# Routed experts of a four-layer decoder: weight buffers addressed by block number, token numbers copied in halves

## The reference

```python
# layer 0: 16 experts, 6 chosen, inner width 176
scores = softmax(h @ gate_w.T); topk_w, topk_idx = top_k(scores, 6)
for e in range(16):
    out = silu(h @ w_gate[e].T) * (h @ w_up[e].T) @ w_down[e].T
    y = y + cw[:, e:e + 1] * out          # cw: the weight of e for each token, 0 where it isn't chosen
# layer 2: 8 experts, 2 chosen, inner width 176, and a shared expert of width 704 with a sigmoid gate
# layer 3: 64 experts, 4 chosen, inner width 96, weights normalised over the chosen
```

## Time and profile before

| | us |
|---|---|
| median of 3 runs (lowest, highest) | 2009.03 (2002.38, 2015.11) |
| profiled execution, its own time | 2001.86 |
| its span, first to last instruction | 2000.0 |
| TensorE busy | 1134.1 |
| VectorE busy | 1150.5 |
| GpSimd busy | 573.5 |
| ScalarE busy | 474.0 |
| mean granted TensorE clock | 0.81 |
| DMA moved | 196.52 MB, 98 GB/s over the span |

### The profile page before, as it was taken

The page is one execution under the profiler, slowest core; times in us unless marked ns, Lnnn a source line. Parts: engine busy times, 40 slices in busy tenths (PEclk is TensorE's granted clock), DMA queues, the critical chain, the costliest instruction groups (busy, mean ns, idle before and its releaser), DMA issues. The chain is left out here.

```text
span 2000.0 us, 21530 instructions
## 1 busy us (share of the span) xinstructions
PE 1134.1 (57%) x5620; PEld 709.2 (35%) x5620; DVE 1150.5 (58%) x2019; ACT 474.0 (24%) x881; POOL 573.5 (29%) x578
## 2 busy tenths in 40 slices
PE   5325537887035773552597803698647278647760
PEld 2201124555023551111354602575424134425550
DVE  5759974333345446898976595421357478483333
ACT  2143301221002344330211100332121156312220
POOL 0026603331730111762200073033212032014425
PEclk9669967999567895897798856899878589869985
DMA  6024334886305502341000011205600510267863
GB/s 203 0 87 147 105 107 139 247 258 213 105 21 128 64 2 87 115 136 63 0 1 0 0 12 31 86 1 150 190 24 0 155 38 3 67 186 231 234 189 102
DMA packets 146194, 196.52 MB, mean 98 GB/s; under 512 B 35056, under 2 KB 109955, under 8 KB 145485
## 3 DMA queue, kind: packets, MB, share of 16 engines
q1 hardware_dynamic: 109996, 144.47, 24.4%
q0 software_dynamic: 12608, 31.26, 5.8%
q10 hardware_dynamic: 23520, 19.93, 3.1%
HBM read 153.55 MB, written 41.75 MB: 98 GB/s over the span
## 5 line engine op out<-in xcount | busy, mean ns | idle before, releaser
L163 PE MATMUL psum<-w_ident,h 128*128 128x128 f32 x144 | 32.7, 422 | 183.3 <-DVE h L144 183.3
L453 PE MATMUL psum<-l0s_conv_out,w_ident 128*128 128x512 f32 x128 | 65.0, 633 | 83.4 <-DVE l0s_conv_out L550 83.4
L453 PE MATMUL psum<-l1s_conv_out,w_ident 128*128 128x512 f32 x128 | 65.3, 636 | 80.0 <-DVE l1s_conv_out L550 80.0
L1471 DVE TENSOR_REDUCE l3x_neg<-psum 128x2 f32<-128x512 f32 x128 | 80.9, 684 | 49.5 <-PE psum L1343 49.5
L925 PE MATMUL psum<-l0f_w_in,l0f_xT 128*128 128x352 f32 x224 | 82.1, 491 | 26.1 <-issue 12.2
L163 PEld LDWEIGHTS psum<-w_ident,h 128*128 128x128 f32 x144 | 29.1, 223 | 186.7 <-DVE h L144 174.5
L175 ACT ACTIVATE hT<-psum 128x512 f32<-128x512 f32 x40 | 21.7, 595 | 304.4 <-PE psum L163 262.7
L1446 ACT ACTIVATE l3x_work<-psum 128x512 f32<-128x512 f32 x128 | 72.5, 599 | 65.3 <-PE psum L1365 65.0
L419 POOL TENSOR_TENSOR l1s_xpad<-l1s_du,l1s_bc 128x1024 f32<-128x1024 f32 x32 | 75.3, 2353 | 32.5 <-DVE psum L546 32.3
L419 POOL TENSOR_TENSOR l0s_xpad<-l0s_du,l0s_bc 128x1024 f32<-128x1024 f32 x32 | 75.2, 2352 | 32.5 <-DVE psum L546 32.4
L152 POOL TENSOR_SCALAR rstd<-moments 128x8 f32<-128x8 f32 x12 | 2.9, 239 | 281.1 <-DVE moments L140 281.1
(11 more groups left out here) (604 smaller groups left out, 3238.5 us busy)
## 6 DMA issues: line engine op xcount, KB each, us to landing
l0f_w_in<-in_l0f_w_in SPq DMA_DIRECT2D x56, 352.0 KB, 4.9
l0s_bc<-l0s_scratch SPq DMA_DIRECT2D x16, 1024.0 KB, 5.2
l1s_bc<-l1s_scratch SPq DMA_DIRECT2D x16, 1024.0 KB, 5.2
l3f_w_in<-in_l3f_w_in SPq DMA_DIRECT2D x64, 192.0 KB, 3.8
l0f_w_down<-in_l0f_w_down SPq DMA_DIRECT2D x56, 176.0 KB
l2f_w_in<-in_l2f_w_in SPq DMA_DIRECT2D x24, 352.0 KB, 4.3
l3f_y_rows<-h SPq DMA_DIRECT2D x16, 512.0 KB, 7.1
l3f_y_rows<-l3f_y ACTq DMA_DIRECT2D x64, 128.0 KB, 3.5
```

What stands on the lines that cost most here:

```text
L163: ins = nc.tensor.transpose(m.psum[:, at:at + P], m.h[:, t, k * P:(k + 1) * P], m.ident[:])
L453: ins = nc.tensor.matmul(m.pair(2 + c)[:, cols], lhsT=m.ident[:], rhs=rhs[:, cols], start=start, stop=stop, skip_group_check=True)
L1471: ins = nc.vector.tensor_reduce(self.neg[k % 2][:, :, hl], bank[:, 0:self.keys].rearrange("p (q k) -> p q k", q=self.maxima), AX_X, ALU.ma ...
```

## The change

`experts` gets an argument `ahead`: 16 for l0f and l2f, 32 for l3f.

- `w_in` and `w_down` become one tile each with `ahead` places; block b lies in place b mod `ahead`. SP fills the first `ahead` blocks in code that is written out (in l2f the last four of these places hold the shared experts first, so only their blocks wait for these), then loops, waiting for the product of the block `ahead` back. In front of each load it also waits until the last load on the same semaphore (four blocks back) has landed. The place in the tile is computed from the block number in a register, by SP for the destination and by TensorE for the operand in its loop; TensorE's first group keeps fixed addresses.
- `token_now` becomes two tiles of two columns. After the second gather of a pair GpSimd waits for the landing of the other pair's earlier gathers and copies that pair's next two columns. `token_of` is two columns longer, cleared by one memset.
- A semaphore `may_load` is counted up and never waited for.

```diff
-    token_of = sb(tag + "token_of", [P, BLOCKS], U32)
-    token_now = sb(tag + "token_now", [P, GROUP], U32)
+    token_of = sb(tag + "token_of", [P, BLOCKS + 2], U32)
+    token_now = ring("token_now", [P, 2], 2, U32)
...
-    w_in = ring("w_in", [P, KD, 2 * F], GROUP)
-    w_down = ring("w_down", [rows, chunks, D], GROUP)
+    w_in = sb(tag + "w_in", [P, ahead, KD, 2 * F])
+    w_down = sb(tag + "w_down", [rows, ahead, chunks, D])
+    place = lambda b: b & (ahead - 1)
+    shared_place = lambda e: ahead - shared + e
...
             def step(base, s, first, last):
                 e = sp.value_load(owners[0:1, bass.ds(base + s, 1)], min_val=0, max_val=E - 1)
                 for w, name, used, loaded in ((w_in, "w_in", in_done, in_loaded), (w_down, "w_down", down_done, down_loaded)):
-                    if first and shared:
-
+                    if first and shared and base + s >= ahead - shared:
                         sp.wait_ge(s_in if w is w_in else s_down, UNITS - shared + s + 1)
                     if not first:
-                        sp.wait_ge(used, base + (s - GROUP + 1))
-                    sp.dma_start(w[s][:].rearrange("p c x -> p (c x)"), source(name, e)).then_inc(loaded[s], 16)
-            by_steps(sp, groups, step, 0)
+                        sp.wait_ge(used, base + (s - ahead + 1))
+                        sp.sem_inc(may_load, 1)
+
+                    if not first or base or shared:
+                        sp.wait_ge(loaded[s], base * (16 // GROUP) + (16 if shared else 0))
+                    sp.sem_inc(may_load, 1)
+                    sp.dma_start(w[:, bass.ds(place(base + s), 1), :, :].rearrange("p o c x -> p (o c x)"), source(name, e)).then_inc(
+                        loaded[s], 16)
+            for g in range(ahead // GROUP):
+                for s in range(GROUP):
+                    step(g * GROUP, s, True, False)
+            with sp.Fori(ahead // GROUP, groups) as i:
+                for s in range(GROUP):
+                    step(i * GROUP, s, False, False)
...
-            def step(base, s, first, last):
-                if s == 0:
-                    if not first:
-                        for k in range(GROUP):
-
-                            pool.wait_ge(x_loaded[k], base * (16 // GROUP))
-                    nc.gpsimd.tensor_copy(token_now[:], token_of[:, bass.ds(base, GROUP)]).then_inc(token_ready, GROUP)
-                    pool.wait_ge(token_ready, base + GROUP)
+            nc.gpsimd.tensor_copy(token_now[0][:], token_of[:, 0:2]).then_inc(token_ready, 1)
+
+            def next_tokens(i, s, first):
+
+                half = (s + 1) // 2 % 2
+                if half == 0 or not first:
+                    for k in range(2):
+                        pool.wait_ge(x_loaded[2 * half + k], i * 16 + (16 if half == 0 else 0))
+                        pool.sem_inc(may_gather, 1)
+                nc.gpsimd.tensor_copy(token_now[half][:], token_of[:, bass.ds(i * GROUP + s + 1, 2)]).then_inc(token_ready, 1)
+
+            def gather(i, s, first):
+                pool.wait_ge(token_ready, i * 2 + (1 + (s + 1) // 2 if s % 2 == 0 else (s + 1) // 2))
+                pool.sem_inc(may_gather, 1)
                 if not first:
-                    pool.wait_ge(x_turned, base + (s - GROUP + 1))
+                    pool.wait_ge(x_turned, i * GROUP + (s - GROUP + 1))
                     pool.sem_inc(may_gather, 1)
                 nc.gpsimd.indirect_dma_start(
-                    x[s][:], None, h_rows, bass.IndirectOffsetOnAxis(ap=token_now[:, s:s + 1], axis=0)).then_inc(
+                    x[s][:], None, h_rows, bass.IndirectOffsetOnAxis(ap=token_now[s // 2][:, s % 2:s % 2 + 1], axis=0)).then_inc(
                         x_loaded[s], 16)
-            by_steps(pool, groups, step, 0)
+                if s % 2:
+                    next_tokens(i, s, first)
...
                     for k in range(KD):
-                        ins = nc.tensor.matmul(in_ps[d % 2], lhsT=xT[d % 2][:, k, :], rhs=w_in[d % GROUP][:, k, :],
+                        ins = nc.tensor.matmul(in_ps[d % 2], lhsT=xT[d % 2][:, k, :], rhs=w_in[:, bass.ds(place(base + d), 1), k, :].rearrange("p o x -> p (o x)"),
                                                start=(k == 0), stop=(k == KD - 1))
```

More of the change, by code:

```diff
@@ L608, in by_steps, with experts @@
         step(groups * GROUP, s, False, True)
-def experts(m, n, j, tag, routed, top, rows, chunks, shared=0, normalize=False, floor=None):
+def experts(m, n, j, tag, routed, top, rows, chunks, ahead, shared=0, normalize=False, floor=None):
     nc = m.nc
@@ L726, in shared_tensor @@
             for k in range(KD):
-                ins = nc.tensor.matmul(s_in_ps[u % 2], lhsT=m.hT[:, k, t * P:(t + 1) * P], rhs=w_in[e][:, k, :],
+                ins = nc.tensor.matmul(s_in_ps[u % 2], lhsT=m.hT[:, k, t * P:(t + 1) * P], rhs=w_in[:, shared_place(e), k, :],
                                        start=(k == 0), stop=(k == KD - 1))
@@ L745, in shared_tensor @@
             for c in range(chunks):
-                ins = nc.tensor.matmul(s_y_ps[t % 2], lhsT=gatedT[u % 2][:, c, :], rhs=w_down[e][:, c, :],
+                ins = nc.tensor.matmul(s_y_ps[t % 2], lhsT=gatedT[u % 2][:, c, :], rhs=w_down[:, shared_place(e), c, :],
                                        start=(e == 0 and c == 0), stop=(e == shared - 1 and c == chunks - 1))
@@ L794, in _ @@
             for e in range(shared):
-                sp.dma_start(w_in[e][:].rearrange("p c x -> p (c x)"), source("w_in", routed + e)).then_inc(in_loaded[e], 16)
-                sp.dma_start(w_down[e][:].rearrange("p c x -> p (c x)"), source("w_down", routed + e)).then_inc(
+                at = shared_place(e)
+                sp.dma_start(w_in[:, at, :, :].rearrange("p c x -> p (c x)"), source("w_in", routed + e)).then_inc(in_loaded[e], 16)
+                sp.dma_start(w_down[:, at, :, :].rearrange("p c x -> p (c x)"), source("w_down", routed + e)).then_inc(
                     down_loaded[e], 16)
@@ L825, in _ @@
             pool.wait_ge(h_stored, 16)
[L827 to L834 removed]
+            nc.gpsimd.tensor_copy(token_now[0][:], token_of[:, 0:2]).then_inc(token_ready, 1)
[9 more added lines that the diff above has]
+                pool.sem_inc(may_gather, 1)
                 if not first:
[L836 removed]
+                    pool.wait_ge(x_turned, i * GROUP + (s - GROUP + 1))
                     pool.sem_inc(may_gather, 1)
                 nc.gpsimd.indirect_dma_start(
[L839 removed]
+                    x[s][:], None, h_rows, bass.IndirectOffsetOnAxis(ap=token_now[s // 2][:, s % 2:s % 2 + 1], axis=0)).then_inc(
                         x_loaded[s], 16)
[L841 removed]
+                if s % 2:
+                    next_tokens(i, s, first)
+            for s in range(GROUP):
+                gather(0, s, True)
+            with pool.Fori(1, groups) as i:
+                for s in range(GROUP):
+                    gather(i, s, False)
             for s in range(GROUP):
@@ L943, in step @@
                     for c in range(chunks):
-                        ins = nc.tensor.matmul(y_ps[d % 2], lhsT=gatedT[d % 2][:, c, :], rhs=w_down[d % GROUP][:, c, :],
+                        ins = nc.tensor.matmul(y_ps[d % 2], lhsT=gatedT[d % 2][:, c, :], rhs=w_down[:, bass.ds(place(base + d), 1), c, :].rearrange("p o x -> p (o x)"),
                                                start=(c == 0), stop=(c == chunks - 1))
@@ L1003, in _ @@
             o.mark(nc.vector.memset(before[:, 0, :], 0.0))
+            o.mark(nc.vector.memset(token_of[:, BLOCKS:], 0.0))
             o.mark(nc.vector.tensor_copy(counting[:], iota[:]))
@@ L1075, in _ @@
             dve.wait_ge(tabled, K)
-            nc.vector.tensor_copy(token_of[:], table).then_inc(table_ready, 1)
+            nc.vector.tensor_copy(token_of[:, 0:BLOCKS], table).then_inc(table_ready, 1)
             o.link(dve, nc.vector.tensor_copy(slot_index[:], slot[:]))
@@ L2259, in decoder @@
             lambda n, j: state_space(m, 0, n),
-            lambda n, j: experts(m, n, j, "l0f_", routed=16, top=6, rows=88, chunks=2),
+            lambda n, j: experts(m, n, j, "l0f_", routed=16, top=6, rows=88, chunks=2, ahead=16),
             lambda n, j: softmax_attention(m, n, j, "l1a_", heads=16, causal=True),
@@ L2265, in decoder @@
             lambda n, j: context_mixing(m, n, j),
-            lambda n, j: experts(m, n, j, "l2f_", routed=8, top=2, rows=88, chunks=2, shared=4, normalize=True),
+            lambda n, j: experts(m, n, j, "l2f_", routed=8, top=2, rows=88, chunks=2, ahead=16, shared=4, normalize=True),
             lambda n, j: gated_recurrence(m, n, j),
             lambda n, j: softmax_attention(m, n, j, "l3x_", heads=32, causal=False),
-            lambda n, j: experts(m, n, j, "l3f_", routed=64, top=4, rows=96, chunks=1, normalize=True, floor=1e-12),
+            lambda n, j: experts(m, n, j, "l3f_", routed=64, top=4, rows=96, chunks=1, ahead=32, normalize=True, floor=1e-12),
         ]
```

4 lines of the change are left out of this document (2 added, 2 removed).

## The result

The changed kernel took 1949.88 us (median of 4 runs, 1929.99 to 1957.7) against 2011.44 for the kernel before, measured beside it: a ratio of 0.9689, 95% interval 0.9639 to 0.9739. A second series (`after_again`) gave 1940.77 against 2006.43, 0.9646 (0.9599 to 0.9693). The forecast was 1943, 66 us less; the medians fell by 62 and 66.

The account below looks back on a forecast made before the run. It took weights arriving late to bound l0f and the gathers' cycle to bound l3f. Gains of 30 (l0f), 6 (l2f) and 30 (l3f) made 66 us, from 2009.0 to 1943; own range 1925 to 1960.

Parts of the forecast that it names:

- The two waits that the forecast named: GpSimd's for gather landings (53.3 us in l0f, 53.9 in l3f); the weights', with SP awaiting TensorE 66.6 us in l0f.
- l0f, forecast 30 (36.2 - 2 - 4): In l0f, 53 steps at 2.49 us instead of 3.17 gain 36.2, less 2 at the start and 4 for stalls.
- The 4 us of stalls: Taken off l0f's gain because DMA at 137 us nearly ties with TensorE's 139; bounds 0 to 16.
- The start cost: The third gather of l0f stands behind a token copy, 2 us later at the stage's start.
- l2f, forecast 6: In l2f, 18 steps fall from 52.2 to 44.8 us, a gain of 7.4, less 1 at the start.
- l3f, forecast 30: In l3f, gains of 26.5 from shorter groups and 5.8 from the tail, less 2 at the start.
- the forecast's formula: A pair's gather cycle: landing + 0.2 + 1.04 + 1.27; 6.8 us a group at landing 4.3, 7.6 assumed at 5.1.
- The tail before: In l3f, from the last token copy to the last output copy's end: 20.6 us before, 14.8 expected after.
- SP, forecast hidden by 11 us: In l3f SP takes 2.1 us per looped block; its last load lands at 1896 against a need at about 1907.
- The rival with a slow SP: At 2.5 us a block l3f ends some 10 us late: gain 54, 1955 us; decides from 2.4; chance 0.07.
- TensorE's addresses, forecast nothing: Some 0.2 us a block of register work on TensorE's queue, hidden as it runs ahead; 14 us if uncovered.
- The DMA rival: DMA engines become the bound in the expert loops: gain only 44 us, 1965 us; chance 0.15.

Follow-up runs that it names:

- after_again: The changed kernel, unaltered, run again in a second series beside the kernel before: 1940.77 us, ratio 0.9646.
- mixed: The changed kernel with 8 places in l0f and l2f and 32 in l3f: 1931.92 us, ratio 0.9633 to the kernel before.
- lean: As mixed, but SP's value load has no run-time bounds check: 1928.55 us, ratio 0.9639 to the kernel before; repeated, 1931.79 us, 0.9623.
- sp_extra: The changed kernel with SP reading each block's owner twice in its loop: 1965.51 us, ratio 0.98 to the kernel before.
- pe_address: The kernel before with only TensorE's w_in and w_down operands addressed by register, SP's code unchanged: 2011.16 us, ratio 1.0015.
- part 2 alone: The changed kernel's token copies in halves, with the old ring of four weight buffers: 2013.06 us, ratio 0.9973 to the kernel before.
- part 1 alone: The changed kernel's 16 or 32 weight places and register addresses, with the old token copies: 1988.81 us, ratio 0.9848 to the kernel before.
- singles: As lean, with token numbers copied one at a time, two blocks ahead: 1931.83 us, ratio 0.9601 to the kernel before.

## Why the prediction was right

The two waits that the forecast named were the ones that mattered, both had to go together, and the sum was 66 us where the three stages gained 67.8. Its terms, one by one, from the first pair of profiles:

- **l0f, forecast 30 (36.2 - 2 - 4), measured 28.5.** The step was right to the hundredth, 53 x 2.49. Two sizes beside it were off and nearly cancelled. The 4 us of stalls did not come inside the loop: TensorE was busy for 80.00 of 80.00 us while the gathers landed in 5.2 to 6.8 us, because the cycle of a pair with that, at most 6.8 + 0.2 + 1.04 + 1.27 = 9.3 us, is shorter than four blocks of TensorE, 9.96. The start cost was put at 2 us, for a copy in front of the third gather. From the stage's start to the third block's input product it went from 58.1 to 66.4 us, 8.3 more; 3.1 of it lies in owners that were known later in this profile. In the second one they were known at 25.4 us, as before, and the third product was only 3.7 us late, but the next steps lost another 3.6: 7 to 8 us either way. That is the mechanism that the forecast missed: the preloads fill the DMA engines just when the first four gathers leave. `mixed` took it away and won 8 us.
- **l2f, forecast 6, measured 8.2.** The start cost of 1 us is not seen, else as reckoned.
- **l3f, forecast 30, measured 34.0.** The gathers' span went from 144.9 us (1783.5 to 1928.4) to 115.8 (1763.9 to 1879.7), 29.1 with the start cost in it, and what lies behind the last gather from 71.6 to 66.7. The group took 7.4 us and not 7.6, and that this is so near is in part luck. By the forecast's formula the landing of 4.6 us would have given 7.1, and the formula for GpSimd's own work 6.9. The second was the larger part: 6.8 of own work, with 0.6 of waiting on top, since in some pairs the one is longer and in some the other. The tail before was read 0.45 us short (the row at 1943.35 holds two copies and ends at 1944.25).
- **SP, forecast hidden by 11 us, measured 1.0 us of waiting, none in the second profile.** The estimate of 2.1 us a block was for two waits and two additions; the loop took 2.44 in the mean, and the bounds check of the value load alone is 0.33 of that, by the 2.10 of `lean`. The rival with a slow SP said that it decides from 2.4 us, and there, in the first profile, the last load did come just too late. Its price was wrong by its own numbers: at 2.5 us the load is 13 us later, which a margin of 11 leaves at 2, not 10. `sp_extra`, with 3.02, shows the price of a slower SP, 18 us.
- **TensorE's addresses, forecast nothing: right,** by `pe_address` (1.0015, 0.9988 to 1.0042). The Trainium skill ("TensorE: Matmul & The Clock Gate", its table of specifications) gives the queue a depth of 64, and this agrees with it; no run here measures the depth.
- **The DMA rival.** It took 285 GB/s as the ceiling, and that was its wrong step: 310 were moved for 80 us. The Trainium skill ("DMA: Bandwidth & Descriptors", the section on the semaphore's 16 increments) has w_down's 88 rows on 11 engines, and the traces agree: in the kernel before each load of l0f's w_in gives 16 semaphore events, each of w_down 12, one some 0.5 us after the issue and eleven as data land. The 151 us that the forecast worked out by it rest on the same 285. From the first input product to the end of the last (324.06 to 463.01) l0f took 139 us, as TensorE's steps have it, at 263 GB/s in the mean. In no run did the amount of data hold up this loop, so none tells what the uneven split costs. One sign of this rival did show: the forecast named landings over 6 us as proof that it was wrong. They were 6.1 in l0f, and it was not. The other signs came as written: copies 3.69 us apart in l3f, a DMA share of 0.85 and 0.87 in the loops. A landing is no loss while the cycle that holds it is shorter than the engine it feeds.
- **Not foreseen: the parts do not add.** The forecast had the gain of part 2 alone at about 30; alone it gained nothing clear of noise (0.9973, 0.9944 to 1.0002), and part 1 alone some 30. The sum was made for both at once, so this did not harm it.
- **Bounds.** Two lower ends do not follow from the terms: stalls of 0 to 16 us leave l0f at 18 to 34, not 16 to 36, and l3f with landings of 5.8 is 16 in the bounds and 19 in the DMA rival. The measured 28.5 and 34.0 lie inside either way.

The end-to-end time agrees with the forecast, 1943, in the second series (1940.77) better than in the first (1949.88), in whose profile l3x, 14 us longer than in the profile before, hid part of the gain. In the 80 us in which l3x packs its q and k, the DMA engines moved 113 GB/s at a share of 0.53, and 120 at 0.41 in the profile before: the same transfers took longer. Why they do so in one execution and not in the next stays open. It happens with the kernel before too (221.0 and 227.8).

## What to carry to other kernels

When two chains close the same loop (here a ring of weights and a chain of gathers), cost each with the other in place: one alone may give little or nothing. A deeper ring moves the bound to the engine that issues the loads, so count its queue's steps (value load, bounds check, waits, two issues, and its share of the branch) against the step it must keep, by their mean and not their median. When a wait is gone, add up the instructions of the engine that waited: they can be the next bound, and a row that names another engine beside an idle time need not mean that it was waited for. Fill ahead as far as the loop's issue rate requires and no further: loads that are not needed yet delay the small ones that start the loop.

## What the runs showed of the hardware

- In l3f SP needed 2.44 us in the mean (2.35 in the median) for a looped block of two loads of 0.35 us each, one value load (0.27 us in the median, 0.44 in l0f) and its waits; 0.33 of it is the bounds check, by the 2.10 of `lean`.
- A mix of weights, gathers and stores kept 310 GB/s for 80 us at a DMA share of 0.99, with no wait on TensorE.
- The first four gathers of 128 rows in l0f landed in 2.7 to 3.0 us while SP issued no loads (`mixed`), in 6.9 to 7.5 while it preloaded sixteen blocks.
- A load of 88 rows (w_down in l0f and l2f) gave 12 semaphore events, one some 0.5 us after the issue; loads of 128 rows (w_in in l0f) gave 16, the first some 3 us after it.
- From a copy of token numbers to the gather that reads them GpSimd took 1.12 us at the least in l3f (30 times); to a gather that reads others (`singles`) 0.71 in the mean.
- A matmul operand addressed by register costs TensorE nothing that 12 executions could tell from a fixed one (1.0015, 0.9988 to 1.0042).
